# Three programs made one in a two-layer decoder, with eight expert slots ahead of the router's end and the third matrix on ScalarE's queue

## The reference, cut to what matters

```
x = x + attn0(ln(x))                 # channel attention
x = x + xattn0(ln(x), context)       # 32 heads
x = x + quantised_linear(ln(x))
x = x + linear_attn(ln(x))           # 16 heads, decay
x = x + conv(context, context, ln(x))# long convolution of products
x = x + moe_block(ln(x))
# moe_block(h0): h  = h0 + attention(rmsnorm(h0))   16 query heads of 128, 4 key heads, rope, causal
#                out = h + sum over the 2 chosen of 8 experts:
#                      w_e * ((silu(t @ w1[e]) * (t @ w3[e])) @ w2[e]),  t = rmsnorm(h), F = 512
```

## Time and profile before

| | |
|---|---|
| median of three runs | 1260.15 us |
| the profiled execution | 1259.27 us |
| its span, first to last instruction | 1257.2 us |
| mean granted TensorE clock | 0.972 |
| PE busy | 1144.3 us, 91% |
| PEld busy | 882.4 us, 70% |
| DVE, ACT, POOL busy | 62%, 44%, 48% |
| mean DMA rate over the span | 79 GB/s |

### The profile page before, as it was taken

How to read it: one execution, slowest core, us unless ns; L and a number is a source line. 1 busy time by engine, 2 the same in 40 slices (tenths; PEclk the granted TensorE clock), 3 DMA queues, 4 the chain that set the end, 5 groups by cost and what they waited for, 6 DMA issues and landing times. The chain is left out here.

```text
span 1257.2 us, 26135 instructions
## 1 busy us (share of the span) xinstructions
PE 1144.3 (91%) x8173; PEld 882.4 (70%) x8174; DVE 775.7 (62%) x1914; ACT 549.3 (44%) x1466; POOL 603.2 (48%) x752
## 2 busy tenths in 40 slices
PE   8998989969999799879999999999999849999996
PEld 5775556635555434358887888888888639999996
DVE  5555788868888589936667667767766432222221
ACT  3444766643333100036666666566666412222221
POOL 2003565536555467455566666656665312233233
PEclk9999999999999889979999999999999869999998
DMA  7000000008994040030000000000000038888884
GB/s 280 0 1 9 14 18 13 9 2 179 205 206 86 1 173 1 1 138 1 5 14 14 18 14 13 21 13 13 13 14 18 21 130 235 232 241 237 235 243 98
DMA packets 57268, 99.86 MB, mean 79 GB/s; under 512 B 5808, under 2 KB 44016, under 8 KB 56432
## 3 DMA queue, kind: packets, MB, share of 16 engines
q1 hardware_dynamic: 48048, 83.37, 23.6%
q0 software_dynamic: 7152, 9.34, 4.3%
q10 hardware_dynamic: 2000, 6.29, 1.3%
HBM read 87.53 MB, written 30.48 MB: 94 GB/s over the span
## 5 line engine op out<-in xcount | busy, mean ns | idle before, releaser
L1922 PEld LDWEIGHTS ga.pkq<-ga.xnT,g.early 128*128 128x128 f32 x1280 | 151.4, 193 | 9.6 <-issue 8.2
L1922 PE MATMUL ga.pkq<-ga.xnT,g.early 128*128 128x128 f32 x1280 | 156.8, 276 | 1.0 <-ACT ga.halves L1840 1.0
L1699 POOL TENSOR_TENSOR ga.halves<-ga.halves,g.ga_sinT 128x512 f32<-128x512 f32 x80 | 103.0, 1287 | 53.0 <-ACT ga.halves L1840 53.0
L1966 PE MATMUL ga.turn_out<-g.early,ga.aT 128*128 128x256 f32 x512 | 117.0, 382 | 0.5 <-ACT ga.aT L1862 0.5
L1847 ACT ACTIVATE ga.e<-ga.psc,ga.negmax 128x128 f32<-128x128 f32 x256 | 90.4, 365 | 48.7 <-DVE ga.negmax L1768 47.7
L1707 POOL TENSOR_TENSOR ga.kqT<-ga.by_cos,ga.halves 128x512 f32<-128x512 f32 x80 | 102.2, 1278 | 15.9 <-issue 15.9
L1966 PEld LDWEIGHTS ga.turn_out<-g.early,ga.aT 128*128 128x128 f32 x512 | 94.9, 190 | 12.3 <-ACT ga.aT L1862 0.7
L1755 DVE TENSOR_TENSOR ga.by_cos<-ga.pkq,g.ga_cosT 128x512 f32<-128x512 f32 x80 | 55.3, 691 | 74.3 <-PE ga.pkq L1922 43.3
L2081 DVE TENSOR_TENSOR ex.hT<-ex.silu,ex.p 128x512 f32<-128x512 f32 x39 | 26.8, 688 | 112.2 <-PE ex.p L2132 106.4
L2125 PEld LDWEIGHTS ex.p<-ex.xnT,ex.w 128*128 128x128 f32 x624 | 77.3, 195 | 5.5 <-issue 2.6
L2125 PE MATMUL ex.p<-ex.xnT,ex.w 128*128 128x128 f32 x624 | 77.8, 279 | 3.0 <-DMA ex.w<-in_mo_w 2.2
(11 more groups left out here) (289 smaller groups left out, 2586.7 us busy)
## 6 DMA issues: line engine op xcount, KB each, us to landing
ex.w<-in_mo_w SPq DMA_DIRECT2D x78, 512.0 KB, 4.5
mo_rows<-in_pad_rows SPq DMA_DIRECT2D x1, 18447.0 KB, 100.9
ex.row<-mo_rows SPq DMA_DIRECT2D x39, 129.0 KB, 3.3
g.late<-in_mo_w SPq DMA_DIRECT2D x1, 4096.0 KB, 12.3
g.ctxT<-in_ctxR SPq DMA_DIRECT2D x1, 2048.0 KB, 13.3
xa.ctxT<-in_ctxT SPq DMA_DIRECT2D x16, 128.0 KB, 2.5
g.spare<-cv_rows SPq DMA_DIRECT2D x1, 2048.0 KB, 8.2
g.early<-in_ga_wq ACTq DMA_DIRECT2D x1, 2048.0 KB, 7.9
```

The costliest lines, as they stand in the source:

```text
L1699: nc.gpsimd.tensor_tensor(by_sin[:, par, :].rearrange("p (h t) -> p h t", h=REP), halves[:, par, :].rearrange("p (h t) -> p h t", h=REP), ...
L1922: last = nc.tensor.matmul(pkq[:, par, j * P:(j + 1) * P], w[:, q, at * P:(at + 1) * P], xnT[:, s.par, q, :], start=(q == 0), stop=(q == C ...
L1966: last = nc.tensor.matmul(pout, aT[:, h // REP, (h % REP) * P:(h % REP + 1) * P], g.ga_wo[:, h, :], start=(h == 0), stop=(h == H - 1))
```

## The change

**One program.** `front_stages`, `grouped_attention` and `experts` become one block, `all_stages`. PSUM is one tensor cut into eight banks, and semaphores of the first two stages are cleared and used again for the experts. Around the convolution's end the attention's first sequence is prepared inside the units: statistics at unit 20, six root parts at units 22 to 27, normalisation at unit 28, transposition at unit 30. Its five parts are then interleaved with the eight turn-backs, and in step 1 the first parts of sequence 1 are moved forward. ScalarE loads the exponential's table ahead (`warm`).

**Early slots.** In step 14 TensorE counts the first 11 sequences (`count_early`) and VectorE makes tables for eight slots that these fill (`early_ends`, `early_tables`). In steps 16 to 18, where no new sequence starts, the products of slots 0, 1 and 2 are put between the attention's (`between`); slots 3 to 7 follow while `tables` makes the entries from 8 on. SP's last stores of x stand between the loads of slots 0 to 3; GpSimd's third expert step and later ones wait for the last two stores (`acc_late`). The expert buffers lie in the space that the convolution has left.

**Third matrix.** ScalarE reads the expert's number and starts w3 of slot t+2 after the silu of slot t and before it copies the rows of slot t+1. All 39 slots remain, with the same products and the same bytes.

```diff
+def steps_from(eng, emit, at, lead, lag, count):
+    last = at + (count - lead - at) // 2 * 2
+    with eng.Fori(at // 2, last // 2) as k:
+        emit(At(2 * k, 0, count))
+        emit(At(2 * k, 1, count))
...
+    def sync(sp):
+        sp.wait_ge(g.cv.z_ready, UNITS - 8)
+        router.load(sp)
+        sp.wait_ge(g.cv.o_turned, B)
+        sp.dma_start(g.mo_w2, g.h["mo_w2"]).then_inc(g.mo_loaded, 16)
...
+        steps(sp, step, 0, 0, count=B - 4, first=2)
+        load = ex_load(sp)
+        router.early_rows_sent(sp)
+        sp.wait_ge(router.early_table, 1)
+        load(At(None, 0, TILES))
+        load(At(None, 1, TILES))
+        step(At(None, B - 4))
+        step(At(None, B - 3))
+        step(At(None, B - 2))
+        load(At(None, 2, TILES))
+        load(At(None, 3, TILES))
+        step(At(None, B - 1))
+        for t in range(4, EARLY):
+            load(At(None, t, TILES))
+        router.rows_sent(sp)
+        sp.wait_ge(router.table, 1)
+        steps_from(sp, load, EARLY, 0, 0, TILES)
...
+        between = {B: (turn_first, first_of_first, turn_second_and_product),
+                   B + 1: (second_slot,),
+                   B + 2: (third_rows, lambda: first_product(slot(2)), lambda: second_product(slot(2)))}
...
+        def rest(turn_back):                       # TensorE
+            first = At(None, 0)
+            values_of(first)
+            pe.wait_ge(g.cv.z_ready, UNITS - 1)
+            kq(first, 0)
+            turn_back(0)
+            kq(first, 1)
...
+            steps(pe, step, 1, 4, start=1)
+            router.count(pe)
+            turn_rows(slot(3))
+            last_product(slot(1))
+            ex_step(slot(3))
+            steps_from(pe, ex_step, 4, 1, 1, TILES)
...
+        def ex_step(t):                            # ScalarE
+            n, n2 = t.back(-1), t.back(-2)
+            if t.on:
+                silu(t)
+            if n2.on:
+                load_third(n2)
+            if n.on:
+                turned_rows(n)
...
+        def load_third(t):
+            expert = act.value_load(g.tile_expert[0:1, bass.ds(t.i, 1)], min_val=0, max_val=E - 1)
+            if t.past(2):
+                act.wait_ge(h3_done, upto(t, back=2))
+            act.dma_start(w3[:, t.par:t.par + 1, :], g.h["mo_w3"][:, bass.ds(expert, 1), :, :].rearrange("p e c f -> p e (c f)")).then_inc(w3_loaded[t.par], 16)
...
-        front_stages(nc, g)
-        grouped_attention(nc, g)
-        experts(nc, g)
+        all_stages(nc, g)
```

More of the change, by code:

```diff
@@ L68, in upto_half, with steps @@
     return 16 * (at.n // 2 + 1) if at.base is None else at.i * 8 + (16 - 8 * at.par)
-def steps(eng, emit, lead, lag, count=B, first=None):
+def steps(eng, emit, lead, lag, count=B, first=None, start=None):
     first = first or (lag + 3) // 2 * 2
     last = first + (count - lead - first) // 2 * 2
-    for s in range(-lead, first):
+    for s in range(-lead if start is None else start, first):
         emit(At(None, s, count))
     with eng.Fori(first // 2, last // 2) as k:
+        emit(At(2 * k, 0, count))
+        emit(At(2 * k, 1, count))
+    for s in range(last, count + lag):
+        emit(At(None, s, count))
+def steps_from(eng, emit, at, lead, lag, count):
+    last = at + (count - lead - at) // 2 * 2
+    with eng.Fori(at // 2, last // 2) as k:
         emit(At(2 * k, 0, count))
@@ L936, in linear_attention @@
     H, HD = 16, 16
-    m = g.la = Names(nc, room, "la")
+    m = g.la = Names(nc, ctx, "la", room)
     xn = m.sb("xn", [P, 2, D])
@@ L1681, in _ @@
         def _(sp):
-            router.load(sp)
-            sp.dma_start(g.mo_w2, g.h["mo_w2"]).then_inc(g.mo_loaded, 16)
-            def step(s):
-                if s.on:
-                    router.store_sum(sp, s)
-            steps(sp, step, 0, 0, count=B - 2, first=2)
-            for b in range(B - 2, B):
-                step(At(None, b))
-            sp.wait_ge(router.acc_stored, 16 * B)
+            ca_sync(sp)
+            xa_sync(sp)
+            la_sync(sp)
+            ga_sync(sp)
@@ L1829, in _, with unit @@
-            steps(dve, step, 2, 4)
-            router.tables(dve)
+            cv = cv_vector(dve)
+            ga_stats, ga_norm, ga = ga_vector(dve)
+            def unit(u):
+                cv(u)
+                if u == ROOT_AT - 2:
+                    ga_stats(At(None, 0))
+                if u == UNITS - 4:
+                    ga_norm(At(None, 0))
+            four_stages(dve, ca_vector(dve), xa_vector(dve), la_vector(dve), unit, late=2)
+            ga(lambda k: add_back(dve, k, 1))
@@ L1909, in _ @@
[L1909 removed]
+            four_stages(act, ca_scalar(act), xa_scalar(act), la_scalar(act), nothing)
+            cv_scalar(act)
+            ga_scalar(act)
         @block.tensor
         def _(pe):
[L1913 to L1924 removed]
```

1281 lines of the change are left out of this document (764 added, 517 removed).

## The result

| | before | after |
|---|---|---|
| median of the runs beside each other | 1260.01 us (1258.65 to 1260.41) | 1228.43 us (1227.95 to 1229.00) |
| span of the profiled execution | 1257.2 us | 1226.5 us |

The ratio is 0.9751, with a 95% interval of 0.9734 to 0.9768. The forecast was 1218 us with a range of 1208 to 1233: the direction and the range hold, and 10.4 us of the expected 42 did not come.

The account below looks back on a forecast made before the run. TensorE was taken to bound the steady stages, with about 40 us of idle time, costed in two seams, to win: 1259.27 - 19 - 25 + 2 = 1217.3, put at 1218 us, range 1208 to 1233.

Parts of the forecast that it names:

- seam one: Convolution to attention: 19 us gained (from 10 to 20 or 22), the engines' meeting removed and the first sequence prepared early.
- Seam two: Attention to experts: 25 us gained (17 to 28), as slots 0 to 2 fill TensorE's waits.
- the sum's price: Attention to experts: two extra ScalarE table loads counted at 1 us together, a load showing as 1.28 us without further gap.
- Rival 3: Early slots start late, SP's first loads standing behind stores and GpSimd's sends; 1231 us, chance 0.04.
- rival 2: Both seams: the drain stays a chain, engines hold each other up, seams give about their lower ends; 1233 us, chance 0.13.
- The third matrix: Expert slots: ScalarE starting w3 moves its copy of the next rows by about 0.3 us, hidden; 0 gain.
- the edge that I had put at 0.9 us: Expert slots: ScalarE's room between ending its copy of the next rows and TensorE wanting them, 0.9 us.
- Rival 1: Expert slots: ScalarE becomes the bound, TensorE waits about 0.4 us a slot, +14 us, 1232 us; chance 0.10.
- Rival 4: Expert slots: w3 on its own queue slows GpSimd's adds, a slot takes 6.99 us, 51 us more, 1269 us; chance 0.03.
- The chain I followed: Convolution to attention: GpSimd's five ropes and two roots, 18.3 us from 531.1, end last; sequence 1 begins at 550.
- The early table: Step 14: some 20 short VectorE operations, about 4 us, delay what queues behind; 1 us lost (0 to 5 with peeled code).
- The 1 us for peeled code: Smaller terms: 1 us lost for more peeled code, part of the 2 us lost in all.

Follow-up runs that it names:

- the spread kernel: Changed kernel with the early table's work spread over steps 14 and 15 where VectorE idles, TensorE's wait moved to slot 0's last product: 1221.67 us, ratio 0.9709.
- the straight line of 96: Changed kernel with 96 small VectorE operations in a straight line behind the last slot, and 96 more in a loop: 1271.05 us, a single time.

## Why the forecast was right, and where it was short

By the spans 42 us were forecast and 30.7 came, 11.3 fewer: 10.4 were missing in seam one and 6.5 in step 14, and 3.0 more than forecast came in seam two and 2.6 in stretches that the forecast held to be unchanged. That the time lies inside the range owes something to luck: without those last 5.6 us it would have been 1234.

**Seam two, 25 forecast, 28.0 measured: right.** The mechanism is the one given: slots 0 to 2 fill the waits of steps 16 to 18. Step 17 began 22.16 us after step 16 (24.85 before; I had taken 1 us, 2.7 came), step 18 12.0 us later (12.2 forecast), and slot 3 9.3 us after that (10.6 forecast). The three table loads that stand there (1000.14, 1008.11, 1010.64) take 1.28 us each; where nothing else was waited for, the next operation starts 0.01 us behind, so the sum's price was right. The run without the fill shows that the fill, and not the early table, carries 17 us of it. Rival 3 falls, and rival 2 for this seam; its other half, a first seam at its lower end, came true.

**The third matrix, 0 forecast: right.** The copy is 0.36 us later (0.3 forecast) with no wait of TensorE; with two transfers the edge that I had put at 0.9 us is reached. Rival 1 was close by, not wrong in kind. Rival 4 did not occur: the slots stay 5.52 us apart on either queue, though the adds land in 4.8 us in the median, against 4.5 with the matrix back on SP's. One step of the working was loose: a copy that ends at 1156.4 is not too late for 1156.48; the 0.3 us holds only with the semaphores' time, which the prediction counts under rival 1 and not there.

**Seam one, 19 forecast, 8.6 measured: the step that failed.** The chain I followed, GpSimd's ropes, is in the main the right one, as the run without turn-backs bears out: 3 us less work of TensorE moved the projection by 0.9 to 1.4. Its terms were too small:
- The convolution: I added 1.4 us to it, so its last product would start at 526.6; it started at 530.4, 3.8 later. 1.5 of this is an offset already there at its first product (which stands anywhere from 442.2 to 445.4 in the profiles of the kernels after it, so it is not the change's). The norm behind unit 28 took 1.82 us where I priced 0.43, TensorE's transposition waited for it, and the units behind it ran at a lower clock:

```profile
521.27 1.82 DVE L1864 TENSOR_SCALAR ga.xn<-g.x,ga.mv,ga.rms 128x256 f32<-128x256 f32 x1
```

```profile
523.24 0.66 PE L2202 MATMUL bank<-g.ident,ga.xn 128*128 128x128 f32 x2 [2.27 <-DVE ga.xn L1864]
523.70 1.92 PE L1354 MATMUL bank<-g.spare 128*128 128x512 f32 x2
525.40 1.56 PE L1355 MATMUL bank<-g.spare 128*128 128x512 f32 x2
526.80 1.02 PE L1356 MATMUL bank<-g.spare 128*128 128x512 f32 x2
```

- From there to the first rope 5.5 us instead of 4.5; the five ropes and two roots, with the wait for ScalarE behind them, 20.8 us instead of the 18.9 up to 550: another 2.9 us in all. With the 3.8 this is the 6.8 us between 550 and 556.76.
- From the first rope of sequence 1 to the first projection I took the time of before, 14.3 us, without saying so; it takes 18.1 now. Statistics, hidden rows and norm of sequence 2 stand ahead of the maxima there, and ScalarE waits for them. The hidden rows take 1.00 us instead of 0.41, beside GpSimd's rope. That this order is the cause is read from the trace; no run moved these three:

```profile
560.15 0.37 ACT L1986 ACTIVATE ga.e<-bank,ga.negmax 128x128 f32<-128x128 f32 x1 [2.85 <-DVE ga.negmax L1840]
```

6.8 and 3.7 are the 10.4 us missing in this seam, to rounding. I left out a comparison that would have shown it: TensorE has 37.3 us of work between the convolution and the first projection, and my marks, from 526.6 to 564.4, gave it 37.8. The forecast needed a TensorE without a wait in a stretch that I myself described as a chain on three other engines. Even the lower end, 10, was not reached, since it went by the idle time removed and held no new waits.

**The early table, 1 forecast (0 to 5), 8.5 measured: the other step that failed.** I counted 4 us of VectorE work and set it against an engine "busy 62%". In step 14 the order decides, not the share: the batches stand ahead of the two things that TensorE waits for next. The 4 us were too few as well: the 21 operations keep VectorE busy for 7.2 us, and for 3.1 in the spread kernel, where none falls beside GpSimd's ropes. The spread kernel has the same operations and pays nothing. The 1 us for peeled code did not show: the peeled step 15 takes 27.66 us, and step 14 with its batches moved 27.97, against 28.02 in the steady steps.

Sum: 8.6 + 28.0 - 8.5 and 2.6 of small differences (1.4 in the steady steps, 1.2 in step 15, their cause open) are 30.7, the difference of the spans (1257.2 to 1226.5).

## What to carry to other kernels

Work that is moved onto an engine with free time costs what stands behind it in that engine's queue; look up which operation the bound engine waits for next, and put the new work behind that one, in pieces the size of the idle times, and away from the operations of an engine that slows it. When two stages are run into each other, check the forecast of the seam against the bound engine's own work in it: if the marks leave it no idle time, they are too early. Before moving a wait, ask whether the instruction behind it waits for the same producer anyway.

## What the runs showed of the hardware that was not expected

Small VectorE operations that take 0.15 us in most places take 1.1 to 1.3 in a few, and the norm 1.82. In the trace after, 36 of VectorE's scalar operations, copies and casts take over 0.3 us more than the shortest of their operation and shape, and 35 of them end within 0.2 us of the end of a GpSimd operation. GpSimd's timeline in the kernel after:

```profile
521.06 1.89 POOL L1266 TENSOR_TENSOR g.spare<-g.ctxT 128x1024 f32<-128x1024 f32 x1 [0.68 <-PE bank L1356]
...
923.09 1.27 POOL L1743 TENSOR_TENSOR ga.halves<-ga.halves,g.ga_sinT 128x512 f32<-128x512 f32 x1 [0.59 <-ACT ga.halves L1979]
924.77 1.30 POOL L1751 TENSOR_TENSOR ga.kqT<-ga.by_cos,ga.halves 128x512 f32<-128x512 f32 x1 [0.41 <-issue]
...
941.27 1.26 POOL L1743 TENSOR_TENSOR ga.halves<-ga.halves,g.ga_sinT 128x512 f32<-128x512 f32 x1 [1.35 <-ACT ga.halves L1979]
```

```profile
941.43 1.13 DVE L1578 CAST g.tile_row<-ga.start_f 128x8 int32<-128x8 f32 x1
```

The norm at 521.27 ends at 523.09, GpSimd's product at 522.95; the operations at 923.12 and 925.00 end at 924.39 and 926.09, GpSimd's at 924.36 and 926.07; the cast at 941.43 ends at 942.56, GpSimd's at 942.53. All of these are scalar operations, copies or casts with SBUF on both sides. An operation with two inputs in SBUF can be slowed too: in the trace with the matrix back on SP's queue L1562, 0.15 us long in the kernel after, takes 1.24 and ends 0.03 us behind GpSimd's. Not every overlap costs: L1536 at 924.78, 0.01 us behind the start of GpSimd's at 924.77, takes 0.15 us.

Two experiments took the neighbour away and left VectorE's operations: behind the convolution the same norm takes 0.41 us, and in the spread kernel all 21 table operations take 0.15 to 0.23. In the straight line of 96 the only GpSimd tensor operation beside them lasts 0.18 us, and none of the 96 took over 0.5 us. The Trainium skill (SBUF — State Buffer, section Who interferes with whom) says that such forms can use a pair of ports that VectorE shares with GpSimd, and that whoever issues first then has it for its whole instruction; the trace agrees, by these ends. By that rule the norm should have been priced at 0.4 us or at what is left of GpSimd's 1.89 us operation. So it is shown that the neighbour makes these operations slow; that the shared ports are how it does so is the page's word, and no run here shows them.

The other surprise is TensorE's clock behind short pauses. After pauses of 3.98 and 2.92 us the profiled kernel after ran on at clock 1.00 in step 15, and the same steps in two other profiles, behind pauses of the same lengths, at 0.90, for 2.9 us more. A pause of TensorE costs its own length in one execution and more in the next.
